# Feed-forward of a hybrid layer: feature rows written once per part, the high rows read twice, reads split in halves and moved, normalisation in two halves

## The reference, cut to what matters

```python
def _layernorm(x, axis=-1, eps=1e-05):
    m = jnp.mean(x, axis=axis, keepdims=True)
    v = jnp.var(x, axis=axis, keepdims=True)
    return (x - m) / jnp.sqrt(v + eps)
...
gate_w = spline_reconstruct(gate_cp, INTER, HIDDEN)   # 1024 x 256 from 2033 control points
up_w = spline_reconstruct(up_cp, INTER, HIDDEN)
down_w = spline_reconstruct(down_cp, HIDDEN, INTER)
gate = jnp.einsum('bsh,ih->bsi', hidden_states, gate_w)
up = jnp.einsum('bsh,ih->bsi', hidden_states, up_w)
inter = jax.nn.silu(gate) * up
return jnp.einsum('bsi,hi->bsh', inter, down_w)
```

## Time and profile before

| | |
|---|---|
| median of 3 runs | 833.07 us |
| the profiled execution | 834.41 us, span 832.7 us |
| mean granted TensorE clock | 0.971 |
| busy: TensorE, VectorE, ScalarE, GpSimd | 93%, 75%, 59%, 29% of the span |
| DMA queue of SyncE | 68848 packets, 108.47 MB |
| reads of `stk` | 128 DMAs of 252 KB |
| writes of `fx` | 48 DMAs high and low (32 of 512 KB, 16 of 504 KB), 48 of the high rows alone (32 of 256 KB, 16 of 252 KB) |
| stores of the result in the loop | 7 of 512 KB |

### The profile page before, as it was taken

One profiled execution on the slowest core, in us unless ns is written; L12 is line 12 of the kernel. 1 busy time (PEld: TensorE's weight loads), 2 busy tenths in 40 slices (PEclk: granted clock), 3 DMA queues, 4 the chain that ended last, 5 costly groups with the idle time before them and its releaser, 6 DMA issues.

```text
span 832.7 us, 19301 instructions
## 1 busy us (share of the span) xinstructions
PE 772.9 (93%) x6818; PEld 661.5 (79%) x6818; DVE 625.8 (75%) x1269; ACT 493.9 (59%) x967; POOL 244.1 (29%) x321
## 2 busy tenths in 40 slices
PE   7789999999999999779999989999999879999988
PEld 7667777777777777559989878998888859988887
DVE  5677777777787788557887768689887667777765
ACT  3145555555554556565666656678887746666643
POOL 4056743222223233311100010166566470000000
PEclk9899999999999999869999999999999989999999
DMA  6765557666586456675666630000043135777731
GB/s 166 115 135 88 93 100 114 97 96 93 87 147 99 80 81 98 210 260 206 232 238 238 236 132 2 1 2 0 2 149 142 38 142 194 273 264 262 261 131 52
DMA packets 70983, 111.48 MB, mean 134 GB/s; under 512 B 7061, under 2 KB 27958, under 8 KB 70854
## 3 DMA queue, kind: packets, MB, share of 16 engines
q1 hardware_dynamic: 68848, 108.47, 49.3%
q10 hardware_dynamic: 2048, 1.88, 1.1%
HBM read 41.82 MB, written 42.81 MB: 102 GB/s over the span
## 4 chain that ended last, share of the span: by engine, by line
PE 54%; DVE 12%; DMA 10%; SPq 9%; issue 9%; ACT 6%; ACTq 0%; DVEq 0%; POOL 0%; POOLq 0%
PE bank L417 8%; PE bank L419 7%; PE bank L418 7%; DMA stk<-fx 5%; PE pair_a L923 5%; SPq L607 4%; PE bank L937 3%; PE pair_b L892 3%; DVE inter L1968 3%; DMA fx<-fs 2%; PE pair_a L1228 2%; SPq L490 2%; DVE spline L2046 2%; PE pair_a L1173 2%; ACT gact L1547 2%
## 5 line engine op out<-in xcount | busy, mean ns | idle before, releaser
L417 PE MATMUL bank<-wd_hi,in_hi 128*128 128x256 f32 x512 | 147.0, 287 | 0.9 <-DVE in_lo L1973 0.8
L419 PE MATMUL bank<-wd_hi,in_lo 128*128 128x256 f32 x512 | 146.1, 285 | 0.0
L418 PE MATMUL bank<-wd_lo,in_hi 128*128 128x256 f32 x512 | 145.9, 285 | 0.0
L1790 DVE TENSOR_REDUCE mx<-pair_b 128x6 f32<-128x768 f32 x124 | 117.9, 951 | 34.4 <-PE pair_b L904 32.2
L1555 ACT ACTIVATE in_hi<-inter 128x512 fp32r<-128x512 f32 x128 | 80.7, 631 | 105.6 <-DVE inter L1968 101.6
L683 POOL TENSOR_SCALAR_AFFINE_SELECT prob<-prob 128x512 f32<-128x512 f32 x128 | 82.1, 642 | 201.4 <-ACT prob L1390 201.3
L1390 ACT ACTIVATE prob<-pair_a 128x768 f32<-128x768 f32 x128 | 103.6, 810 | 63.0 <-PE pair_a L923 61.2
L1973 DVE TENSOR_TENSOR in_lo<-inter,in_hi 128x512 fp32r<-128x512 f32 x128 | 89.0, 695 | 60.9 <-ACT in_hi L1555 59.4
L417 PEld LDWEIGHTS bank<-wd_hi,in_hi 128*128 128x128 f32 x512 | 98.3, 192 | 6.2 <-DVE in_lo L1973 1.7
L418 PEld LDWEIGHTS bank<-wd_lo,in_hi 128*128 128x128 f32 x512 | 98.2, 192 | 4.8
L419 PEld LDWEIGHTS bank<-wd_hi,in_lo 128*128 128x128 f32 x512 | 98.1, 192 | 0.0
(11 more groups left out here) (233 smaller groups left out, 1960.3 us busy)
## 6 DMA issues: line engine op xcount, KB each, us to landing
stk<-fx SPq DMA_DIRECT2D x128, 252.0 KB
stack<-stage SPq DMA_DIRECT2D x184, 128.0 KB, 4.4
fx<-fs SPq DMA_DIRECT2D x32, 512.0 KB, 3.6
fx<-fs SPq DMA_DIRECT2D x32, 256.0 KB, 3.8
fx<-fs SPq DMA_DIRECT2D x16, 504.0 KB
fx<-fs SPq DMA_DIRECT2D x16, 252.0 KB
X<-in_attn_a_x SPq DMA_DIRECT2D x14, 256.0 KB, 5.4
result<-X SPq DMA_DIRECT2D x7, 512.0 KB, 8.0
```

The lines of the kernel that those rows point to most:

```text
L417: pe.matmul(dst, l_hi, r_hi, start=first, stop=False)
L418: pe.matmul(dst, l_hi, r_lo, start=False, stop=False)
L419: return pe.matmul(dst, l_lo, r_hi, start=False, stop=last)
L1790: dve.tensor_reduce(mx[:, h, :, p % PR, :], src[:, :, 0:3 * P].rearrange("p n (t k) -> p n t k", t=3), AX.X, ALU.max).then_inc(a_mx, 1)
```

## The change

`fx` holds two copies, high and low, and each slot is written by one DMA. A read of block m becomes two DMAs: six kinds of 14 rows (high, low) to partitions 0 to 83, and three kinds (the high rows again) to partitions 84 to 125. Reads have two halves, blocks 0 to 3 and 4 to 7, with a semaphore for each parity and half. Half 1 of group g + 1 is read in period g behind `write_x(g + 2)`; half 0 of group g + 2 is read in period g too, behind `write_moments(g + 2)`, when four up matmuls of group g are done. TensorE waits for half 0 at m = 0 and for half 1 at m = 4. The reads of groups 0 and 1 stand ahead of the loops. `normalise4` does two of its tiles at m = 4 and two at m = 5.

```diff
@@ -279,7 +279,7 @@
 
 
         wdx = nc.dram_tensor("wdx", [INTER + 1, D], F32, kind="Internal").ap()
-        fx = nc.dram_tensor("fx", [2, 3 * FROWS + P, 2 * S], F32, kind="Internal").ap()
+        fx = nc.dram_tensor("fx", [2, 2 * FROWS + P, 2 * S], F32, kind="Internal").ap()
 
 
         s_x = [sem(f"x_loaded{n}") for n in range(4)]
@@ -363,8 +363,9 @@
             f.gp, f.upp, f.dp = own("gp", MT), own("upp", MT), own("dp", MT + 1)
             f.pe = [f.xT, f.mp, f.gp, f.upp, f.dp]
 
-            f.xw, f.mw, f.ld = own("xw", 64), own("mw", 32), own("ld", 16 * MT)
-            f.sp = [f.xw, f.mw, f.ld]
+            f.xw, f.mw = own("xw", 32), own("mw", 16)
+            f.ld = [[own(f"ld{u}{half}", 8 * MT) for half in range(2)] for u in range(2)]
+            f.sp = [f.xw, f.mw] + f.ld[0] + f.ld[1]
             return f
 
         f_ = ffn_semaphores()
@@ -573,23 +574,24 @@
                 if b in (1, 2):
                     sp.wait_ge(s_zero, 1)
                     sp.dma_start(copies[b - 1, :, D, :].rearrange("v (p k) -> v p k", k=32),
-                                 zeros[48 * (b - 1):48 * b, :]).then_inc(s_zeros, 16)
+                                 zeros[32 * (b - 1):32 * b, :]).then_inc(s_zeros, 16)
                 if nxt and not nxt2:
                     f1_write_x(0, 0)
                     f1_write_moments(0, 0)
                     load_down(range(KG // 2, KG))
 
-            copies = fx[:, 0:3 * FROWS, :].rearrange("u (v q) t -> u v q t", q=FROWS)
+            copies = fx[:, 0:2 * FROWS, :].rearrange("u (v q) t -> u v q t", q=FROWS)
 
             def ffn(base, store, first):
                 def write(u, slot, at, n, landed):
-                    sp.dma_start(copies[u, 0:2, at:at + n, :].rearrange("v p t -> p v t"),
+                    sp.dma_start(copies[u, :, at:at + n, :].rearrange("v p t -> p v t"),
                                  fs[0:n, :, slot, :].bitcast(F32)).then_inc(landed, 16)
-                    sp.dma_start(copies[u, 2, at:at + n, :], fs[0:n, 0, slot, :].bitcast(F32)).then_inc(landed, 16)
 
                 def write_x(g, u):
                     sp.wait_ge(f_.xl, upto(f_.xl, base + g, CT))
-                    sp.wait_ge(f_.ld, upto(f_.ld, base + g - 2, 16 * MT))
+                    for half in range(2):
+                        sp.sem_inc(passed_sp, 1)
+                        sp.wait_ge(f_.ld[u][half], upto(f_.ld[u][half], base + g - 2 - u, 16 * MT))
                     for c in range(CT):
                         write(u, c, P * c, P, f_.xw)
 
@@ -597,26 +599,30 @@
                     sp.wait_ge(f_.ml, upto(f_.ml, base + g, 1))
                     write(u, CT, 2 + 2 * FSTEP, P - 2, f_.mw)
 
-                def read(g, u):
-                    sp.wait_ge(f_.xw, upto(f_.xw, base + g, 64))
-                    sp.wait_ge(f_.mw, upto(f_.mw, base + g, 32))
-                    sp.wait_ge(f_.upp, upto(f_.upp, base + g - 1, 1))
-                    for m in range(MT):
+                def read(g, u, half):
+                    sp.wait_ge(f_.xw, upto(f_.xw, base + g, 32))
+                    sp.wait_ge(f_.mw, upto(f_.mw, base + g, 16))
+                    sp.sem_inc(passed_sp, 1)
+                    sp.wait_ge(f_.upp, upto(f_.upp, base + g - 2, MT // 2 * (half + 1)))
+                    for m in range(MT // 2 * half, MT // 2 * (half + 1)):
                         at = 2 + KG * m
-                        rows = fx[u, at:at + 9 * FSTEP, :].rearrange("(r q) t -> r q t", q=FSTEP)[:, 0:NB, :]
-                        sp.dma_start(stk[0:NFX, u, m, :].bitcast(F32), rows).then_inc(f_.ld, 16)
+                        for to, kinds in ((0, 6), (2 * NF, 3)):
+                            rows = fx[u, at:at + kinds * FSTEP, :].rearrange("(r q) t -> r q t", q=FSTEP)[:, 0:NB, :]
+                            sp.dma_start(stk[to:to + kinds * NB, u, m, :].bitcast(F32), rows
+                                         ).then_inc(f_.ld[u][half], 16)
 
                 def period(g, u, prev=True, nxt=True, nxt2=True, nxt3=True):
                     if nxt2 and prev:
                         write_x(g + 2, u)
-                    if nxt:
-                        read(g + 1, 1 - u)
+                    if nxt and prev:
+                        read(g + 1, 1 - u, 1)
                     if prev:
                         store(g - 1)
                     else:
                         first()
                     if nxt2:
                         write_moments(g + 2, u)
+                        read(g + 2, u, 0)
 
                 return write_x, write_moments, read, run_pairs(period)
 
@@ -637,16 +643,22 @@
             f1_write_x(1, 1)
             sp.wait_ge(s_zeros, 32)
             sp.wait_ge(a_stp, upto(a_stp, B - 2, NP))
-            f1_read(0, 0)
+            for half in range(2):
+                f1_read(0, 0, half)
             f1_write_moments(1, 1)
             f1_write_x(2, 0)
             sp.wait_ge(a_stp, upto(a_stp, B - 1, NP))
+            for half in range(2):
+                f1_read(1, 1, half)
             run_f1(sp)
             f2_write_x(0, 0)
             f2_write_moments(0, 0)
-            f2_read(0, 0)
+            for half in range(2):
+                f2_read(0, 0, half)
             f2_write_x(1, 1)
             f2_write_moments(1, 1)
+            for half in range(2):
+                f2_read(1, 1, half)
             f2_write_x(2, 0)
             run_f2(sp)
             for h in range(2):
@@ -1167,8 +1179,9 @@
 
                 def period(g, u, prev=True, nxt=True, nxt2=True, nxt3=True):
                     for m in range(MT):
-                        if m == 0:
-                            pe.wait_ge(f_.ld, upto(f_.ld, base + g, 16 * MT))
+                        if m % (MT // 2) == 0:
+                            landed = f_.ld[u][m // (MT // 2)]
+                            pe.wait_ge(landed, upto(landed, base + g - u, 16 * MT))
                         pe.wait_ge(f_.si, upto(f_.si, base + g, m - 1))
                         pe.matmul(pair_a[:, m % 2, :], cst[:, 0, m, :], stk[0:NFX, u, m, :], start=True,
                                   stop=True).then_inc(f_.gp, 1)
@@ -1523,22 +1536,22 @@
             attention = period
 
             def ffn(base, ahead, tail, first):
-                def normalise4(g):
+                def normalise4(g, tiles=range(2 * TB)):
                     act.wait_ge(f_.mr, upto(f_.mr, base + g, 1))
                     act.wait_ge(f_.xT, upto(f_.xT, base + g - 1, CT))
                     act.sem_inc(passed_act, 1)
-                    for t in range(2 * TB):
+                    for t in tiles:
                         act.activation(xr[:, t, :], X[:, bass.ds(2 * TB * g + t, 1), :], ACT.Identity,
                                        bias=fnmr[:, t:t + 1], scale=frs[:, t:t + 1]).then_inc(f_.xn, 1)
 
                 def high_x(g, c, src):
                     act.wait_ge(f_.xT, upto(f_.xT, base + g, c + 1))
-                    act.wait_ge(f_.xw, upto(f_.xw, base + g - 1, 64))
+                    act.wait_ge(f_.xw, upto(f_.xw, base + g - 1, 32))
                     act.activation(fs[:, 0, c, :], src[:, :], ACT.Copy).then_inc(f_.xh, 1)
 
                 def high_moments(g, src):
                     act.wait_ge(f_.mp, upto(f_.mp, base + g, 1))
-                    act.wait_ge(f_.mw, upto(f_.mw, base + g - 1, 32))
+                    act.wait_ge(f_.mw, upto(f_.mw, base + g - 1, 16))
                     act.activation(fs[:, 0, CT, :], src[:, :], ACT.Copy).then_inc(f_.mh, 1)
 
                 def silu(g, m):
@@ -1563,8 +1576,8 @@
                         silu(g, m)
                         if m == BEHIND and nxt2:
                             high_moments(g + 2, bank_t)
-                        if m == 5 and nxt3:
-                            normalise4(g + 3)
+                        if m in (4, 5) and nxt3:
+                            normalise4(g + 3, range(TB * (m - 4), TB * (m - 3)))
                         if m == MT - 1 and nxt3:
                             high_x(g + 3, 0, bank_t)
                             high_x(g + 3, 1, bank_p)
```

## The result

The changed kernel takes 911.93 us, the median of 4 runs, against 832.64 us before in the same session: ratio 1.0935, 95% interval [1.0884, 1.0986]. Of its runs, 907.76, 909.86, 914.01 and 966.93 us, the last had a mean granted clock of 0.734 and is left out of the ratio (the median of the other three is 909.86). The profiled execution has a span of 908.1 us at a mean granted clock of 0.941, against 832.7 at 0.971: 75.4 us longer.

The account below looks back on a forecast made before the run. Three DMA engines serving both pieces of each `stk` read would set the pace. Profiled 834.4 us plus 48.1 and 38.5 for the two feed-forwards, less 1.3 to the median, is 919.7; forecast 919, range 882 to 940.

Parts of the forecast that it names:

- The count of engines: Split `stk` reads: 84 rows get six engines, 42 get three, nested; three engines carry 224 rows a group instead of 112.
- The price of a half: Half read of `stk`, four blocks: 10.0 us on the three engines, with 9.0 and 10.6 kept as bounds.
- The dry gap: Behind each moment write, while SyncE waits for its landing: the three engines run dry for 2.3 us.
- rival (c): In both feed-forwards: engines bind but leftover transfers cover the dry gap, 28 us less, 892; no separate chance, within the range.
- The period: A group on the three engines: 26.9 us in the first feed-forward, 28.3 in the second, against TensorE's 19.3.
- The two chains: Last group's fifth gate matmul comes later: 48.1 us from the first feed-forward, 38.5 from the second.
- The waits: TensorE's waits for `stk`, 5 us and more in nearly all groups: together 80 to 100 us.
- the two slow-clock stretches: Low granted clock, counted by the rival with enough engines as 3.4 us to be gained.
- rival (a): `stk` reads find other engines, not nested or more each; the change gains 15.8 us, giving 817; chance 0.13.
- Normalisation: Two tiles in each of two steps: gain unseen while TensorE waits for `stk`; if uncovered, 0 to -3.1 us.
- SyncE's issues: On SyncE: issues grow from 14 to 19 a group, 15 us at 0.8 each, beside the 26.9 us period.
- Rival (b): During reads: an engine speeds up when few are busy; nothing gained or lost, 833 us; chance 0.03.

Follow-up runs that it names:

- three_by_42: The kernel before, with each read of 126 rows issued as three DMAs of 42 rows; nothing else changed: 1068.51 us, ratio 1.2851.
- after_turned: The changed kernel with the rows of `stk` in the orders 14 x 6 and 14 x 3, 14 outermost: 830.46 us, ratio 0.9992.
- before_turned: The kernel before, whole reads, with the 126 rows in the order 14 x 9 instead of 9 x 14: 826.63 us, ratio 0.9943.
- moved_turned: The changed kernel with whole reads of 126 rows in the order 14 x 9 and three copies: 818.56 us, ratio 0.985.
- once_spread: The changed kernel, each half read by nine DMAs, one per kind, 14 rows x 4 blocks, targets 9 partitions apart: 848.06 us, ratio 1.0176.
- before_by_kind: The kernel before, each group's read as nine DMAs, one per kind, 14 adjacent partitions x 8 blocks: 914.23 us, ratio 1.101.
- by_kind_spread: The kernel before, each group's read as nine DMAs, one per kind, with the 14 target partitions 9 apart: 827.47 us, ratio 0.9953.
- after_by_kind: The changed kernel, each half read by nine DMAs, one per kind, 14 adjacent partitions x 4 blocks: 845.87 us, ratio 1.0184.

## Why the prediction was right

Forecast 919 us, measured 911.9. By its steps:

- *The count of engines (84 rows on six, 42 on three, nested).* Shown: shares of 0.37 and 0.20 in the trace after, and three_by_42 (0.19), where three sets of three are the same three. The count that fits both ends, inferred from nine and fourteen (0.59 and 0.92 in the earlier trace rows), held for six and three too. These four and the sixteen of the writes of 128 partitions (1.02) are the only counts read off a trace here. after_turned is the cross-check: the same DMAs and bytes, with 14 outermost, are 81 us faster.
- *The price of a half.* This was the term that was mis-sized: 10.0 us against 9.4. From 452.3 to 475.8 us the three engines are busy, 23.5 us; less feature write 2.8 and moment write 1.8, each half is (23.5 - 4.6)/2 = 9.4. That lies between the best window of before (9.0; 229 GB/s on nine, 25 each; the earlier trace rows) and the read by its bytes (9.9); in the quiet windows above the three engines moved 25 GB/s each. Why the read at 620.64 ran slower was not looked into.
- *The dry gap.* 2.3 forecast, 2.5 measured (475.8 to 478.3). Nothing covered it, so rival (c) is out.
- *The period.* 26.9 forecast, 25.9 by these terms, and 26.2 between the second halves of groups 1 and 6 in the first feed-forward (396.32 to 527.25, five groups); 28.3 against 27.1 in the second (785.28 to 866.53, three).
- *The two chains.* 48.1 was forecast and 41.5 came, 38.5 and 33.9: about a microsecond a group less. The half's price alone takes off more than that, 16 x 0.6 = 9.6 and 12 x 0.6 = 7.2; the longer dry gap (6 x 0.2 in each) and a period 0.3 longer than its terms in the first give some of it back. Measured, the chains are 11.2 us shorter than forecast, and by the half's price they would be 16.8 shorter: that the terms set too low made up 5 to 6 us of it is luck.
- *The waits.* 80 to 100 us were forecast, 62.4 came. They are 51.7 more than before, of the 75.4 us that the span grew. The forecast took its lengthening for waiting, but part of the time between two transfers TensorE spent slow instead of idle. Ten waits are of 3.8 us and more, 54.9 us together, and behind each the clock is at 0.50 for 3.4 to 6.1 us with TensorE at work. Two of them, from the first gate matmul on:

```profile
463.36:468.00 4.64, 4.64 (x22) 4.35 (x23) 1.68 (x3) 2.09 (x4) 0.00 (x0) 0.62 0.48 167
...
515.46:522.00 6.54, 6.54 (x28) 6.16 (x29) 3.88 (x13) 2.45 (x4) 1.26 (x2) 0.54 0.51 181
```

The clock lacks 0.38 x 4.64 = 1.8 us and 0.46 x 6.54 = 3.0 us of full speed here. By the same sum it is 23 us behind all ten, and 3.3 behind the waits of 2.90 and 2.52 before (the two slow-clock stretches of rival (a), 3.4 there: 0.28 x 6 and 0.34 x 5, from the earlier trace rows): an estimate of 20 of the other 24 us. What is left is small waits: those for `inter` and `gact` grew from 1.6 and 1.0 to 3.8 and 3.0 us, those for `xr` fell by 3.1.
- *Normalisation.* In the changed kernel TensorE waits for `stk` instead, as said; no run has that kernel without the split. But its bounds for when it is uncovered, 0 to -3.1 us, were wrong: alone it gave -0.9% (some 7 us). The step that failed was to price it by the waits of TensorE. The Silu step of the earlier trace rows was the better row: four tiles lengthen it by 0.9 us (2.97 against 2.07). A group is 18.75 us in before_turned and 17.5 with the split, while the list of waits shows only 0.6 us of a group as idle time; that list was too small a measure of it.
- *SyncE's issues.* 15 us a group, hidden beside 26.9: right for this kernel. But rival (a), 817 us with enough engines, was priced without them. after_turned, which is that case, took 830: with two DMAs per block the issues, in one queue with the wait for landing, become the bound. moved_turned has half as many reads, the same waits for landing and more written bytes, and took 818.6.
- *Rival (b)*, engines that speed up when few are busy, did not come: 25 GB/s each at three, 23 to 25 at nine.

What stays open: of target partitions only adjacent ones and ones 9 apart were run, at 119 and 269 GB/s; why adjacent ones are slower, and from what distance on they are not, is not shown. And why a gather with adjacent targets is issued in less time (below) was not tried. That a ring of ScalarE with the other engines makes the 18.75 us of a group is inferred from the Silu step and from what the split gave; the chain through it was not followed.

## What to carry to other kernels

Before a DMA is split or its rows regrouped, find how many engines each piece gets: it can be read off the share in a quiet window (share x 16). Here nine kinds of 14 rows got nine engines (0.59), six kinds six (0.36 to 0.37) and three kinds three (0.19 to 0.20), and the pieces of six and three didn't add up to nine but lay on the same ones. If the count is small because a small number is outermost, turn the order of the rows: with 14 outermost at both ends a read got fourteen (0.83 to 0.87 in moved_turned). Keep the targets of one DMA apart in partitions (9 apart gave 269 GB/s, adjacent ones 119) and its bytes large for each issue (an issue took 0.84 to 0.88 us with 126 KB on the average in after_turned, some 150 GB/s, and 0.84 with 252 KB in moved_turned, 264 to 283 GB/s). And when one limit goes, ask for the next before promising its whole stall: here, with the reads on fourteen engines, ScalarE's work came next (0.8 to 0.9%) and SyncE's issues (1.4% in after_turned, 3.3% in once_spread, against moved_turned). Moving reads behind a wait for a landing needs room on the DMA engines: with nine it cost 0.8%, with fourteen nothing that these runs can tell.

## What the runs showed of the hardware that I had not expected

- DMAs that write into 14 adjacent partitions each moved 119 GB/s on the average (90 to 141) at a share of 0.94 in before_by_kind; into 14 partitions 9 apart, with the same source rows, 269 GB/s (209 to 307) at 0.81 in by_kind_spread.
- The issue of one gather from SyncE costs mostly 0.77 to 0.94 us whether it carries 84, 112 or 252 KB, and only 0.42 to 0.59 us when its 14 targets are adjacent (nine in 3.8 to 5.3 us in after_by_kind):

```profile
764.47 3.76 SPq L611 DMA_DIRECT2D stk<-fx  x9
```

- The wait of 5.40 us before 463.36 was followed by 3.5 us of work at a granted clock of 0.50, about 1.8 us more. Over the ten long waits of the changed kernel it is 23 us on 55: they cost an estimated four tenths more than they show.
